# A fused attention and FP4 feed-forward block: one instruction for the block scales of x and h, the context snapshot between the two tanh, q's transposes and copy at the end of the step

## The reference

```python
xn = layernorm(x)
# attention: buckets of 64 tokens, each sees the sums of the buckets before it
q = softmax(q, axis=-1) * HEAD_DIM ** (-0.5)
k = exp(k)
context = exclusive_cumsum(einsum('bhnsd,bhnse->bhnde', b_k, b_v))
den = einsum('bhnsd,bhnd->bhns', b_q, exclusive_cumsum(b_k_sum))
attn = einsum('bhnsd,bhnde,bhns->bhnse', b_q, context, 1 / max(den, 1e-6))
attention = attn @ W_out.T
# feed-forward: fp4_linear quantises both operands
scale = max(max(abs(block)) / 6, 1e-12)     # a block is 16 neighbours
q = GRID[searchsorted(MID, abs(block / scale))] * sign * scale
h = silu(fp4_linear(xn, w_gate)) * fp4_linear(xn, w_up)
out = x + attention + fp4_linear(h, w_down)
```

## Time and profile before

| | before |
|---|---|
| median of 3 runs | 1361.32 us (1359.19 to 1363.07) |
| the profiled execution, its own time | 1361.72 us |
| its span, first to last instruction | 1360.0 us |
| VectorE busy | 1309.7 us (96%), 3901 instructions |
| TensorE busy | 1271.1 us (93%), 9934 |
| ScalarE busy | 969.4 us (71%), 3221 |
| GpSimd busy | 355.0 us (26%), 791 |
| mean granted TensorE clock | 0.989 |

### The profile page before, as it was taken

How to read it: one execution, slowest core, us unless ns; L and a number is a source line. 1 busy time by engine, 2 the same in 40 slices (tenths; PEclk the granted TensorE clock), 3 DMA queues, 4 the chain that set the end, 5 groups by cost and what they waited for, 6 DMA issues and landing times.

```text
span 1360.0 us, 41012 instructions
## 1 busy us (share of the span) xinstructions
PE 1271.1 (93%) x9934; PEld 871.0 (64%) x9934; DVE 1309.7 (96%) x3901; ACT 969.4 (71%) x3221; POOL 355.0 (26%) x791
## 2 busy tenths in 40 slices
PE   0279999999999999999999999999999999999996
PEld 0157666666666666666666666666666666666664
DVE  6869999999999999999999999999999999999996
ACT  1567777777777777777777777777777777777772
POOL 2212223222222323222222222223232222323220
PEclk9889999999999999999999999999999999999998
DMA  4024544444454444444544444545454454445444
GB/s 129 12 40 82 108 98 100 105 100 102 98 114 100 101 105 98 103 100 98 113 101 105 98 102 99 112 98 104 105 109 99 92 115 101 96 105 110 97 83 91
DMA packets 432380, 133.64 MB, mean 98 GB/s; under 512 B 397404, under 2 KB 431836, under 8 KB 432348
## 3 DMA queue, kind: packets, MB, share of 16 engines
q1 hardware_dynamic: 431622, 132.60, 46.8%
q10 hardware_dynamic: 726, 0.72, 0.2%
HBM read 19.99 MB, written 16.78 MB: 27 GB/s over the span
## 4 chain that ended last, share of the span: by engine, by line
DVE 52%; issue 33%; DVEq 7%; PE 5%; ACT 2%; DMA 1%; SPq 0%; ACTq 0%
DVE hx_v L880 7%; DVE ga L810 5%; DVE blk L834 3%; DVE xring L963 3%; DVE hx_v L887 3%; DVE h L820 2%; DVE drec L794 2%; DVE xq_s L935 2%; DVE q_rows L922 2%; DVE att L799 2%; DVE osum L958 2%; DVE blk L843 1%; DVE dz L786 1%; DVE hrow L854 1%; DVE dmx L790 1%
## 5 line engine op out<-in xcount | busy, mean ns | idle before, releaser
L418 POOL TENSOR_TENSOR xn_s<-xn,xn_s 128x256 f16<-128x256 f32 x128 | 108.6, 848 | 820.3 <-ACT xn_s L535 820.3
L1165 PE MATMUL outp<-w_down_cat,q_rows 128*128 128x256 f16 x1408 | 246.1, 274 | 0.0
L617 ACT ACTIVATE snap<-ctxp,mask 64x68 f32<-64x68 f32 x1024 | 236.5, 310 | 3.3
L1165 PEld LDWEIGHTS outp<-w_down_cat,q_rows 128*128 128x128 f16 x1408 | 138.3, 98 | 16.5
L1167 PE MATMUL outp<-w_down_lo,q_rows 128*128 128x256 f16 x640 | 147.6, 274 | 0.0
L580 ACT ACTIVATE th<-unit0a,c_g 128x352 f32<-128x352 f32 x128 | 71.0, 554 | 97.3 <-PE unit0b L1078 95.3
L556 ACT ACTIVATE qexp<-qsh,c_q 128x256 f32<-128x256 f32 x128 | 65.1, 508 | 99.0 <-DVE qsh L773 98.8
L580 ACT ACTIVATE th<-unit1a,c_g 128x352 f32<-128x352 f32 x128 | 71.0, 555 | 87.4 <-PE unit1b L1078 65.0
L827 DVE TENSOR_REDUCE blk<-h 128x44 f32<-128x704 f32 x128 | 123.8, 967 | 0.1
L411 POOL TENSOR_TENSOR att_s<-att,att_s 128x256 f16<-128x256 f32 x128 | 87.9, 687 | 108.1 <-ACT att_s L572 108.1
L880 DVE TENSOR_TENSOR hx_v<-h,blk 128x704 f32<-128x704 f32 x128 | 111.0, 868 | 0.0
(11 more groups left out here) (199 smaller groups left out, 4059.0 us busy)
## 6 DMA issues: line engine op xcount, KB each, us to landing
xring<-x SPq DMA_DIRECT2D x128, 128.0 KB, 2.7
out<-xring SPq DMA_DIRECT2D x128, 128.0 KB, 2.5
xnt<-xn_s SPq DMA_TRANSPOSE x128, 2.5
xqt<-xq_s SPq DMA_TRANSPOSE x128, 2.4
att_t<-att_s SPq DMA_TRANSPOSE x128, 2.5
q_rows<-q_rows SPq DMA_TRANSPOSE x128, 3.6
raw_qkv<-wqkv_t SPq DMA_DIRECT2D x1, 768.0 KB, 4.4
raw_up<-wup ACTq DMA_DIRECT2D x2, 352.0 KB
```

Of the source, the lines that this page charges most:

```text
L418: nc.gpsimd.tensor_tensor(xn_s[:, par, 1, :], xn[:, par, :], xn_s[:, par, 0, :], ALU.subtract).then_inc(xn_lo, 1)
L617: nc.scalar.activation(kept[:, :, cols], sums[:, :, cols], ACT.Copy, scale=mask[rows, f, h:h + 1])\
L1165: nc.tensor.matmul(downp, hqt[:, par, m, :], w_down_cat[:, m, :], start=(m == 0), stop=False)
```

## The change

It has two parts. In VectorE's `block_scales` the two instructions become one over all 60 columns of `blk`: a `scalar_tensor_tensor` that multiplies by the constant and takes the maximum with a new tile, `blk_floor`, which holds both floors and is filled once in the preparation by two instructions. It counts on a semaphore of its own, `blk_scaled`, so that `xq_step` counts 5 and `hq_step` 8 per tile. And three calls move: ScalarE's `snapshot` from the end of the step to between the two `tanh_gate`, its `copy_qt` from ahead of `squares_of` to the end (with `squares_wait`, a wait for the mean's accumulator, now ahead of `high_xn`), and TensorE's `transpose_q` from ahead of `project_att` to the end of the step.

```diff
+        blk_floor = sb("blk_floor", [P, FB + XB])
...
             def scales_x(t):
-                act.wait_ge(xq_step, after(t, 6, 2))
+                act.wait_ge(blk_scaled, t + 1)
...
             def step(n, d):                       # ScalarE
                 tanh_gate(k, 0, par)
+                snapshot(k + 1)
                 normalise_waits(k + 3)
                 mean_waits(n, d + 4)
                 tanh_gate(k, 1, par)
                 factor_of_row(k - 1, odd)
                 normalise(n, d + 3)
                 mean_of(n, d + 4)
+                squares_wait(k + 4)
                 high_xn(k + 3, odd)
-                squares_wait(k + 4)
+                squares_of(n, d + 4)
                 copy_qt(k + 1, odd)
-                squares_of(n, d + 4)
-                snapshot(k + 1)
...
             def block_scales(t, u):               # VectorE
-                if is_tile(u):
-                    dve.wait_ge(xq_step, after(u, 6, 1))
-                    nc.vector.tensor_scalar(xblk[:, 1, :], xblk[:, 0, :], SIX_TIE * 2.0 ** 11, XS * TINY * 2.0 ** 11, ALU.mult, ALU.max)\
-                        .then_inc(xq_step, 1)
-                if is_tile(t):
-                    dve.wait_ge(hq_step, after(t, 9, 1))
-                    nc.vector.tensor_scalar(hblk[:, 1, :], hblk[:, 0, :], SIX_TIE * 2.0 ** 11, h_floor[:, :], ALU.mult, ALU.max)\
-                        .then_inc(hq_step, 1)
+                do_h, do_x = is_tile(t), is_tile(u)
+                if do_h:
+                    dve.wait_ge(hq_step, after(t, 8, 1))
+                if do_x:
+                    dve.wait_ge(xq_step, after(u, 5, 1))
+                if do_h or do_x:
+                    both = slice(0 if do_h else FB, FB + XB if do_x else FB)
+                    nc.vector.scalar_tensor_tensor(blk[:, 1, both], blk[:, 0, both], SIX_TIE * 2.0 ** 11, blk_floor[:, both],
+                                                   ALU.mult, ALU.max).then_inc(blk_scaled, 1)
...
+            nc.vector.memset(blk_floor[:, FB:FB + XB], XS * TINY * 2.0 ** 11).then_inc(factors, 1)
+            dve.wait_ge(factors, 12)
+            nc.vector.tensor_copy(blk_floor[:, 0:FB], h_floor[:, :].broadcast_to([P, FB])).then_inc(factors, 1)
...
             def step(n, d, ends=False):           # TensorE
                 gate_up(k, 0, par)
                 gate_up(k, 1, par)
-                transpose_q(k + 1, odd)
                 project_att(k - 2, par)
                 project_h(k - 2, par)
+                transpose_q(k + 1, odd)
```

More of the change, by code:

```diff
@@ L208, in linear_attention_fp4_ffn_block @@
         xq_step = sem("xq_step")
+        blk_scaled = sem("blk_scaled")
         hx_step = sem("hx_step")
@@ L295, in turn_xq @@
                     return
-                sp.wait_ge(xq_step, after(t, 6))
+                sp.wait_ge(xq_step, after(t, 5))
                 sp.sem_inc(sp_turn, 1)
@@ L306, in turn_h @@
                     return
-                sp.wait_ge(hq_step, after(t, 9))
+                sp.wait_ge(hq_step, after(t, 8))
                 sp.sem_inc(sp_turn, 1)
@@ L520, in normalise_waits @@
                 if begun(t - 2):
-                    act.wait_ge(xq_step, after(t - 2, 6, 3))
+                    act.wait_ge(xq_step, after(t - 2, 5, 2))
             def normalise(n, d):
@@ L592, in factor_of_row @@
                     return
-                act.wait_ge(hq_step, after(t, 9, 4))
+                act.wait_ge(hq_step, after(t, 8, 3))
                 if begun(t - 2):
@@ L600, in scales_h @@
                     return
-                act.wait_ge(hq_step, after(t, 9, 5))
+                act.wait_ge(hq_step, after(t, 8, 4))
                 nc.scalar.activation(hs_hi[:, :].rearrange("p (b i) -> p b i", i=2), twice(hblk[:, 1, :]), ACT.Copy,
@@ L818, in times_up @@
                 if begun(t - 2):
-                    dve.wait_ge(hq_step, after(t - 2, 9, 6))
+                    dve.wait_ge(hq_step, after(t - 2, 8, 5))
                 nc.vector.tensor_tensor(h[:, par, half * FH:(half + 1) * FH], ga[:, half, :],
@@ L852, in over_one @@
                 if do_h:
-                    dve.wait_ge(hq_step, after(t, 9, 2))
+                    dve.wait_ge(blk_scaled, t + 4)
                     nc.vector.tensor_reduce(hrow[:, 0, :], hblk[:, 1, :], AX.X, ALU.max).then_inc(hq_step, 1)
@@ L856, in over_one @@
                     if do_x:
-                        dve.wait_ge(xq_step, after(u, 6, 2))
+                        dve.wait_ge(blk_scaled, u + 1)
                     both = slice(0 if do_h else FB, FB + XB if do_x else FB)
@@ L862, in row_scale @@
                 if is_tile(t):
-                    dve.wait_ge(hq_step, after(t, 9, 3))
+                    dve.wait_ge(hq_step, after(t, 8, 2))
                     if begun(t - 1):
@@ L871, in over_row @@
                     return
-                dve.wait_ge(hq_step, after(t, 9, 4))
+                dve.wait_ge(hq_step, after(t, 8, 3))
                 nc.vector.reciprocal(hrow[:, 2, :], hrow[:, 1, :]).then_inc(hq_step, 1)
@@ L897, in round_hx @@
                     if do_h:
-                        dve.wait_ge(hq_step, after(t, 9, 6))
+                        dve.wait_ge(hq_step, after(t, 8, 5))
                     if do_x:
-                        dve.wait_ge(xq_step, after(u, 6, 3))
+                        dve.wait_ge(xq_step, after(u, 5, 2))
                     nc.vector.tensor_scalar(hx_u[:, both], hx_v[:, both].bitcast(bf16)[:, 1:2 * (both.stop - both.start):2],
@@ L905, in round_hx @@
                     if begun(t - 1):
-                        dve.wait_ge(hq_step, after(t - 1, 9))
+                        dve.wait_ge(hq_step, after(t - 1, 8))
                     if begun(u - 1):
-                        dve.wait_ge(xq_step, after(u - 1, 6))
+                        dve.wait_ge(xq_step, after(u - 1, 5))
                     nc.vector.tensor_scalar(hx_q[:, both], hx_u[:, both].bitcast(u16), GRID16, -GRID16, ALU.add, ALU.add)\
@@ L920, in scale_h @@
                 else:
-                    dve.wait_ge(hq_step, after(t, 9, 7))
+                    dve.wait_ge(hq_step, after(t, 8, 6))
                 nc.vector.tensor_tensor(rows(hq_s[:, par, part * F:(part + 1) * F]), rows(hx_q[:, 0:F].bitcast(fp16)),
@@ L929, in scale_x @@
                 dve.wait_ge(hx_step, hx_after(t, 3))
-                dve.wait_ge(xq_step, after(t, 6, 4))
+                dve.wait_ge(xq_step, after(t, 5, 3))
                 if begun(t - 2):
@@ L1051, in _ @@
             low_cols()
-            dve.wait_ge(factors, 11)
+            dve.wait_ge(factors, 13)
             for n in range(0, 2):
```

## The result

The changed kernel takes 1366.07 us (median of 8 runs, 1363.26 to 1368.71), the one before 1360.84 in 8 runs beside it (1359.19 to 1363.07). The ratio is 1.0036, its 95% interval 1.0024 to 1.0049: slower by 5.2 us. I had said 1357 and "faster" as the likeliest sign. The time is within the range of 1346 to 1371, the direction is wrong.

A forecast was written before the change was run, and what follows sets the result against it. A two-step loop over TensorE, ScalarE, GpSimd and VectorE was taken as the bound: 14.73 + 0.61 + 3.81 + 0.54 = 19.69 us a pair, 5.0 us saved over 124 steps, hence 1357.1 us, range 1346 to 1371.

The forecast's parts named there:

- the loop: Two-step cycle through TensorE's gates, ScalarE, GpSimd's `low_att`, VectorE's scales, xring and `project_att`: 19.77 us before, 19.69 forecast.
- TensorE's floor: TensorE's own work from one `project_att` to the next, claimed to need 9.77 us a step without waiting.
- the rival at 1348: No time lost between `low_att` and the scaling, so TensorE's 9.77 a step decides: 14.3 us saved; chance 0.22.
- The joined operation: VectorE's single scaling of 60 columns: 0.13 us, bounds 0.10 to 0.22, and GpSimd can hold it up.
- the lock: SBUF ports shared by VectorE and GpSimd: while `low_att` holds them, VectorE's operations with two SBUF inputs wait.
- The transposes: TensorE's two transposes of q, moved behind `project_h`: gates and first tanh 0.30 us later, seen from `project_att`.
- that stretch: From `project_att` to the first tanh: 7.97 us plus 0.30 for q's transposes, 8.27.
- ScalarE's tail: First tanh through snapshot and second tanh to xn_s and `low_xn`: 0.45 + 1.90 + 1.53 + 0.12 + 0.48 us.
- GpSimd's queue: `low_xn` and the four small operations ahead of `low_att`, to the end of shift: 1.98 us.
- the rival of the longer queue: `low_xn` and small GpSimd operations meet VectorE's xq_s products and lengthen: slower, 1372 us at 0.25 more; chance 0.18.
- The lock's release: From `low_att`'s start to qmax, with VectorE let in before `low_att` ends: 0.61 us.
- the pair: Two successive steps together, whose sum alone is fixed: 19.77 us before, 19.69 forecast.

The follow-up runs named there:

- the joined kernel: Only the joined block scaling, the three calls left where they stood in the kernel before: 1385.8 us, ratio 1.0183; with its two waits changed round 1351.6 us.
- the best kernel: Kernel before plus joined scaling with h's wait last, snapshot between the two tanh, and `low_att` ahead of GpSimd's small operations: 1332.3 us, ratio 0.9792.

## Why the prediction was wrong

**What bounds the kernel.** Right. Six kernels that shorten the loop at different links (the snapshot with and without the join, the transposes, xn_s, `low_att`, the order of the waits in the joined kernel) gain 9 to 14 us each over before. The busy times don't put the kernels in order: VectorE is busy for 1309.7 us before, for 1298.5 in the changed kernel, which is slower, and for 1302.7 with the snapshot alone moved, which is 9.9 us faster. With `low_att` ahead of the small operations the scaling is not held.

**TensorE's floor.** Misread. The prediction says: "at 836.75 it starts 0.30 behind the transposes, which is their own length for two, so it waits for nothing". In the earlier trace rows xring starts at 836.21 and `project_att` 0.54 later, which is exactly the latency that I used as a term of the loop. So it did wait, for xring, and the 0.30 held 0.08 of that wait. Their own length is 0.22 (818.17 to 818.39 in the best kernel). The floor is 9.67, so the rival at 1348 stood 12 us too high (124 x 0.10); the kernel that reaches the floor takes 1332.3.

**The joined operation.** Its own length was right, 0.14 against my 0.13, and so was "removing L843 is worth little". What I said of the semaphores, "the waits are as many as before", was true and missed the point: two waits on one instruction, the one that ends last named first, put its start 0.10 later, by the swap. In the changed kernel that costs nothing, since the lock covers it (1366.0 against 1366.1), but alone it decides between 1351.6 and 1385.8.

**The transposes.** 0.30 predicted, 0.27 measured in the rows and 0.24 a pair by experiment. With the rest of that stretch (8.14 in place of 8.27) this term was too large by 0.13 (0.05 in the loop that starts a step later).

**ScalarE's tail.** First tanh to second tanh 2.35, as predicted. From there to `low_xn` 2.23 in place of 2.13: xn_s starts 1.74 behind the second tanh (849.20 to 850.94) where I had 1.53 + 0.12 = 1.65, so the wait for the mean's accumulator costs 0.21, a little more than its upper bound of 0.19, where I had chosen 0.12. Taken back together with the new place of q's copy, as in the kernel with the snapshot moved (1346.5), that wait gives the loop nothing: xn_s stands 1.53 behind the second tanh there, but `low_att` 4.39 behind it, against 4.40 in the changed kernel with its transposes back (1350.3; medians over every second step, 4.31 in both over the others). GpSimd's var_scaled then waits for the squares, which stand behind the copy of q. That way into GpSimd's queue wasn't in my sum.

**GpSimd's queue, the failed step.** The mechanism was right, and this term of the sum was too small. I had "`low_xn` to the end of shift [...] 1.98" with bounds from 0.1 less to 0.41 more, and it measured 2.17 (2.08 in the loop that starts a step later). Two things make it up. From var_scaled to shift it is 1.22 (852.06 to 853.28), and 1.32 in the step before, where var_eps takes 0.34 instead of 0.19 beside xq_s's products (842.27 beside 842.28); those are the meetings that the rival of the longer queue named. And from shift's start to `low_att`'s it is 0.32 in one of the two steps and 0.14 in the other. That alternation, 0.32 and 0.14, is in all eight kernels that have the snapshot moved and the old order on GpSimd. In GpSimd's program the hardware loop's branch stands between shift and `low_att` in every second step, and nothing else differs between the two. The trace of the changed kernel shows that it is the branch back. Four steps stand ahead of the loop, one behind the other in the program, and there `low_att` starts 0.14 behind shift in both kinds of step (0.17 where the loop is entered); where the loop ends and the program goes on without branching back, it is 0.16. GpSimd's timeline, ahead of the loop and at its end:

```profile
88.08 0.19 POOL L438 TENSOR_TENSOR shift<-neg_mean,rstd 128x1 f32<-128x1 f32 x1
88.22 0.67 POOL L413 TENSOR_TENSOR att_s<-att,att_s 128x256 f16<-128x256 f32 x1
...
1311.14 0.19 POOL L438 TENSOR_TENSOR shift<-neg_mean,rstd 128x1 f32<-128x1 f32 x1
1311.30 0.67 POOL L413 TENSOR_TENSOR att_s<-att,att_s 128x256 f16<-128x256 f32 x1
```

In the kernel before, GpSimd stood idle there for 0.55, waiting for ScalarE, so the branch was hidden. That the queue lies on the path is shown by the two kernels that shorten it or the way to it; of its excess of 0.19 the branch makes 0.13 (0.32 where I had 0.19 for shift), and the way from `low_xn` to shift 0.06 (1.85 where I had 1.79). That split is read from rows. That loops have ends which also cost was nowhere in my list of what the change uncovers.

**The lock's release.** From `low_att` to qmax 0.67, predicted 0.61: the joined operation is let in 0.53 behind `low_att`'s start and then takes 0.14. The rule of the Trainium skill (SBUF — State Buffer, section "SBUF: two separate sides") that the first holder keeps the lock for the whole instruction would have made it 0.67 + 0.14 = 0.81; the trace agrees on the lock and not on its length.

**The sum and the chances.** 19.69 became 19.91: -0.13 at the gates, +0.10 in the tail, +0.19 in the queue, +0.06 at the lock. I had written of the longer queue "from 0.15 more in the chain on, the pair passes 19.84 and the kernel is measurably slower", and 0.22 more is that case. A gain of 0.08 a pair was forecast from terms whose bounds alone were 0.19 and 0.5 wide, and the widest, the queue, was taken 0.1 above its lower end. 0.49 for faster was more than that sum could bear. The regular pair alone would have made the change dearer than it is: 19.91 against 19.77 is 0.07 a step, 8.7 us. The prediction left before's few irregular steps as they were (9.906 the mean against 9.885 in the pair, 2.6 us); in the changed kernel they are gone (9.947 against 9.955), and the whole is 5.1.

## What to carry to other kernels

When two engines are both over 90% busy, follow one long loop through the timelines, across steps if the steps' lengths alternate, and spend edits on its links alone: moving one call that the shares call cheap (two transposes of 0.27) cost 1.2% here, and moving another (the snapshot) won 0.7%. Before an edit uncovers an engine's queue, write down everything in that queue, its waits, its small operations and the loop's branch, and where an instruction waits for two semaphores, name last the one that ends last; that gained 34 us in one kernel here and nothing in two others, where the lock took it back. GpSimd's long operation with two inputs belongs beside a VectorE operation with one, a reduction here: with `low_att` there and the scaling joined, the kernel went from 1360.8 to 1332.3 us.

## What the runs showed of the hardware

- VectorE's operation with two inputs in SBUF is let in 0.53 us after the start of GpSimd's 0.67 us subtraction, not at its end (the joined scaling: 0.67 from `low_att` to qmax, less its own 0.14); whoever starts first decides who waits, and 0.09 us ahead was enough (817.51 against 817.60).
- One program has two lasting regimes with steps of 9.88 and 10.21 us on the same chip and clock (granted clock 1.00 in both windows), by the order in which two engines meet at the lock.
- Of two semaphore waits on one instruction, the order of naming moved its start by 0.10 us (1.11 against 1.00 to 1.02 behind the producer's start).
- The read-out of the mean's accumulator lasts 0.19 us. Without a wait for it, xn_s started 1.53 behind the second tanh, with the wait 1.74.
- The branch back of GpSimd's loop put the next operation's start 0.18 us later: 0.32 behind shift's start in place of 0.14.
